# Selective scan on one core: VectorE multiplies the first unit of each block by C, and POOL multiplies whole units in one instruction

## What is computed

```python
x = x + 0.5 * ffn(layernorm(x))
h = layernorm(x)
for p in layers:                      # 4 layers
    xn = rmsnorm(h) * norm_w
    xp, z = split(xn @ Win)           # 256 channels each
    xc = silu(causal_conv(xp))
    dt, Bm, Cm = split(xc @ Wx)       # 64, 16, 16
    delta = softplus(dt @ Wdt + bdt)
    # over 512 steps, 256 channels x 16 states:
    s[t] = exp(delta[t] * A) * s[t-1] + (delta[t] * xc[t]) * Bm[t]
    y[t] = sum_over_states(s[t] * Cm[t]) + xc[t] * Dp
    h = h + (y * silu(z)) @ Wblk
x = x + h @ Wout + bout
x = x + 0.5 * ffn(layernorm(x))       # 8 experts, gate and up of 344 columns
```

## Time and profile before

| | us |
|---|---|
| median of 3 runs | 4576.21 (4574.02 to 4577.95) |
| profiled execution, its own time | 4581.88 |
| its span | 4580.2 |
| POOL busy in the span | 4095.2 (89%) |
| DVE busy | 4067.8 (89%) |
| PE busy | 3945.9 (86%) |
| ACT busy | 3346.7 (73%) |
| mean granted clock of PE | 0.948 of full |

### The profile page before, as it was taken

The page is one execution under the profiler, slowest core; times in us unless marked ns, Lnnn a source line. Parts: engine busy times, 40 slices in busy tenths (PEclk is TensorE's granted clock), DMA queues, the critical chain, the costliest instruction groups (busy, mean ns, idle before and its releaser), DMA issues.

```text
span 4580.2 us, 48320 instructions
## 1 busy us (share of the span) xinstructions
PE 3945.9 (86%) x11712; PEld 1285.4 (28%) x11712; DVE 4067.8 (89%) x5505; ACT 3346.7 (73%) x5047; POOL 4095.2 (89%) x1804
## 2 busy tenths in 40 slices
PE   7886777898998999899898999899899989678869
PEld 2221222232232323232232323223232322122223
DVE  2668898999999999999999999999999999889963
ACT  4566776777777787777778777787777777667744
POOL 0559999999999999999999999999999999999960
PEclk9897887999999999999999999999999999789969
DMA  2234444354435444544454445444434453443410
GB/s 72 58 74 96 112 100 94 88 114 104 94 90 111 97 94 96 114 95 94 98 111 93 89 105 113 92 91 104 111 87 92 109 113 85 98 100 88 93 46 5
DMA packets 137665, 426.06 MB, mean 93 GB/s; under 512 B 15917, under 2 KB 36334, under 8 KB 137007
## 3 DMA queue, kind: packets, MB, share of 16 engines
q1 hardware_dynamic: 137391, 422.97, 40.8%
HBM read 146.09 MB, written 8.39 MB: 34 GB/s over the span
## 4 chain that ended last, share of the span: by engine, by line
POOL 31%; DVE 25%; issue 17%; PE 16%; ACT 9%; DMA 1%; SPq 1%; DVEq 0%; ACTq 0%; POOLq 0%
POOL work L873 18%; POOL work L864 11%; DVE work L685 10%; DVE dA_ps L685 7%; PE d_ps L400 3%; ACT dA_ps L522 2%; DVE work L690 2%; PE a_ps L393 2%; DVE sg_sb L769 2%; ACT L550 2%; PE a_ps L387 2%; PE b_ps L387 1%; PE y_ps L371 1%; PE b_ps L393 1%; PE s_ps L470 1%
## 5 line engine op out<-in xcount | busy, mean ns | idle before, releaser
L873 POOL TENSOR_TENSOR work<-dd_sb,bc_sb 128x2048 f32<-128x2048 f32 x512 | 2318.8, 4529 | 127.1 <-PE y_ps L371 62.1
L522 ACT ACTIVATE dA_ps<-dd_sb,a_sb 128x512 f32<-128x512 f32 x2048 | 1370.7, 684 | 488.2 <-DVE work L690 298.0
L685 DVE TENSOR_TENSOR_SCAN work<-dA_ps,work 128x512 f32<-128x512 f32 x1408 | 1650.7, 1205 | 62.8 <-POOL work L873 36.6
L864 POOL TENSOR_TENSOR work<-work,bc_sb 128x1024 f32<-128x1024 f32 x704 | 1655.7, 2359 | 13.2 <-DVE work L685 11.9
L685 DVE TENSOR_TENSOR_SCAN dA_ps<-dA_ps,work 128x512 f32<-128x512 f32 x640 | 780.8, 1220 | 12.3 <-ACT dA_ps L522 6.1
L400 PE MATMUL d_ps<-sg_sb,wd_sb 128*128 128x512 f32 (+1 forms) x1536 | 728.7, 605 | 44.2 <-DVE sg_sb L769 44.2
L371 PE MATMUL y_ps<-work,sel_sum 128*32 128x512 f32 x4096 | 594.0, 654 | 88.6 <-POOL work L864 56.5
L387 PE MATMUL b_ps<-xT_sb,wg_sb 128*128 128x512 f32 (+1 forms) x768 | 433.9, 647 | 95.9 <-ACT sg_sb L549 91.8
L387 PE MATMUL a_ps<-xT_sb,wg_sb 128*128 128x512 f32 (+1 forms) x768 | 431.5, 644 | 97.1 <-ACT sg_sb L549 96.2
L690 DVE TENSOR_TENSOR work<-dA_ps,bc_sb 128x512 f32<-128x512 f32 x640 | 438.7, 685 | 11.8
L393 PE MATMUL a_ps<-xs_sb,wu_sb 128*128 128x512 f32 (+1 forms) x768 | 419.7, 629 | 20.4 <-DVE sg_sb L769 15.9
(11 more groups left out here) (116 smaller groups left out, 3820.7 us busy)
## 6 DMA issues: line engine op xcount, KB each, us to landing
dd_sb<-dd_src SPq DMA_DIRECT2D x512, 512.0 KB, 8.6
bc_sb<-bc_rows SPq DMA_DIRECT2D x256, 512.0 KB, 5.7
xr_sb<-in_L_attn_x SPq DMA_DIRECT2D x16, 256.0 KB, 2.8
bc_rows<-dbc_sb SPq DMA_DIRECT2D x128, 32.0 KB, 1.7
out<-xr_sb SPq DMA_DIRECT2D x16, 256.0 KB, 2.2
wg_sb<-in_L_ffn_Wg SPq DMA_DIRECT2D x1, 1376.0 KB
wu_sb<-in_L_ffn_Wu SPq DMA_DIRECT2D x1, 1376.0 KB
wd_sb<-in_L_ffn_Wd SPq DMA_DIRECT2D x2, 512.0 KB
```

The lines of the kernel that those rows point to most:

```text
L522: act.activation(dA_ps[:, g % NDA, :], dd_sb[:, b, c, 0, :], ACT.Exp, scale=a_sb[:, l, b, j, c:c + 1]).then_inc(dA_ready, 1)
L685: dve.tensor_tensor_scan(dA if on_dve(i) else tile, dA, tile, 0.0, ALU.mult, ALU.add).then_inc(scanned, 1)
L864: pool.tensor_tensor(work[:, g % RING], work[:, g % RING], bc_sb[:, j, 0, :].unsqueeze(1).broadcast_to([128, 2, T]), ALU.mult).then_inc(po ...
L873: pool.tensor_tensor(work[:, g % RING:g % RING + 2].rearrange("p h c t -> p (h c) t"), dd_sb[:, b, :, 1, :], bc_sb[:, j, 1, :].unsqueeze(1 ...
```

## The change

DVE now takes halves 0 and 1 (unit 0), 5 (second half of unit 2), 8 and 9 (unit 4): ten tiles as before. POOL multiplies units 1, 3, 5, 6 and 7 with one instruction of 128 x 2048 each, and half 4 with one of 128 x 1024. Units 0 and 4 have no POOL product. An instruction for a whole unit waits for all four scans of the unit, where one for a first half waited for two. All tables of offsets are new too; a few of their lines are shown.

```diff
-CORE = {"exp": -10, "scan": -1, "dbu": -1, "dve_prod": 0, "pool_prod": 17, "sum": 30, "y0": 87, "y1": 11}
+CORE = {"exp": -6, "scan": 0, "dbu": 7, "dve_prod": 3, "pool_prod": 27, "sum": 33, "y0": 92, "y1": 15}
...
-DVE_UNITS = (0, 2, 3, 5, 6)
-NDP, NPP = len(DVE_UNITS), HALVES - len(DVE_UNITS)
+DVE_HALVES = (0, 1, 5, 8, 9)
+POOL_HALVES = [[h for h in (2 * u, 2 * u + 1) if h not in DVE_HALVES] for u in range(UNITS)]
+NDP, NPP = len(DVE_HALVES), sum(1 for halves in POOL_HALVES if halves)
...
 def on_dve(i):
-    return i // NG in DVE_UNITS and i % NG >= 2
+    return i // 2 in DVE_HALVES
...
 def dve_products(k, i):
-    return k * NDP + sum(1 for u in DVE_UNITS if 2 * u + 1 <= i)
+    return k * NDP + sum(1 for h in DVE_HALVES if h <= i)
 def pool_products(k, i):
-    return k * HALVES + i + 1 - dve_products(k, i)
+    return k * NPP + sum(1 for halves in POOL_HALVES if halves and halves[-1] <= i)
...
-                if (at := part_at(t, CORE["pool_prod"], 8)) and not (at[2] % 2 == 1 and at[2] // 2 in DVE_UNITS):
-                    k, w, i = at
-                    j, g = (i // 2) % NJ, HALVES * k + i
-                    pool.wait_ge(scanned, 2 * g + 2)
-                    pool.tensor_tensor(work[:, g % RING], work[:, g % RING],
-                                       bc_sb[:, j, 0, :].unsqueeze(1).broadcast_to([128, 2, T]), ALU.mult).then_inc(pool_prod, 1)
+                if (at := part_at(t, CORE["pool_prod"], 16)) and POOL_HALVES[at[2]]:
+                    k, w, u = at
+                    halves = POOL_HALVES[u]
+                    h0, n = (HALVES * k + halves[0]) % RING, len(halves)
+                    tile = work[:, h0:h0 + n].rearrange("p h c t -> p (h c) t")
+                    pool.wait_ge(scanned, 2 * (HALVES * k + halves[-1]) + 2)
+                    pool.tensor_tensor(tile, tile, bc_sb[:, u % NJ, 0, :].unsqueeze(1).broadcast_to([128, 2 * n, T]),
+                                       ALU.mult).then_inc(pool_prod, 1)
```

More of the change, by code:

```diff
@@ L45 @@
-END = {"yt": 17, "xo": 30, "bn": 42, "nb": 69, "xtok": 67, "ht": 80, "h": 79, "store": 119, "acc": 9}
+CORE = {"exp": -6, "scan": 0, "dbu": 7, "dve_prod": 3, "pool_prod": 27, "sum": 33, "y0": 92, "y1": 15}
+PREP = {"dc1": 90, "dc0": 68, "sq": -23, "ms": -13, "rms": -8, "xn": -6, "xp0": 19, "conv0": 21, "xp1": 24, "conv1": 26,
+        "silu_xc": 30, "z0": 39, "zc0": 35, "z1": 51, "zc1": 53, "silu_z": 62, "wx": 43, "dbc": 43, "rows": 1, "dt0": 55,
+        "sp0": 59, "delta0": 62, "du0": 66, "dt1": 69, "sp1": 74, "delta1": 79, "du1": 86, "dd0": 21, "dd1": 110, "bc": 46}
@@ new lines @@
+NEAR = {"dc1": 110, "dc0": 89, "sq": 32, "ms": 37, "rms": 39, "xn": 43, "xp0": 53, "conv0": 54, "xp1": 56, "conv1": 58,
+        "silu_xc": 62, "z0": 65, "zc0": 65, "z1": 70, "zc1": 67, "silu_z": 94, "wx": 72, "dbc": 76, "rows": 23, "dt0": 76,
+        "sp0": 78, "delta0": 84, "du0": 84, "dt1": 91, "sp1": 91, "delta1": 97, "du1": 97, "dd0": 41, "dd1": 60, "bc": 33}
+POST = {"wblk": 93, "h": 92, "attn": 103, "x2": 108}
+POST_NEAR = {"wblk": 29, "h": 35, "attn": 38, "x2": 39}
+FFN_AT = {"gb": 1, "xs": 5, "g0": 7, "g1": 8, "g2": 11, "burst": 8, "u0": 14, "u1": 15, "u2": 18, "hh0": 15, "hh1": 17,
+          "hh2": 24, "down": 37}
@@ L48, in phase_table @@
+START = {"load": -130, "bn": -71, "nb": -46, "xtok": -46, "xt": -37, "xT": -38, "lg": -36, "lg_sb": -37, "mx": -36,
+         "mi": -36, "gap": -24, "we": -26, "eq": -26, "den": -15, "inv": -25, "comb": -8, "ct": -6, "gates": -14}
+END = {"yt": 25, "xo": 29, "bn": 46, "nb": 65, "xtok": 61, "ht": 87, "h": 87, "store": 102, "acc": 16}
 def phase_table():
```

## The result

The changed kernel takes 4788.24 us (4782.37 to 4791.23, three runs) against 4576.21 us: 1.0462 times as long, 95% interval 1.0446 to 1.0479. The forecast was 4750 us, with a range of 4590 to 4860. The profiled execution has a span of 4786.5 us, and in it POOL is busy for 4053.2 us (85%) and DVE for 4068.8 us (85%). DVE has the work that it had. POOL has 42 us less, nearly the 48 us that fewer instructions should save, and yet the kernel is 212 us slower.

A forecast was written before the change was run, and what follows sets the result against it. POOL set the pace, with DVE nearly as full; after the change a loop between them makes phases 68.0 us, 68.7 with the router, against 65.7. 58 x 3.0 = 174 us on 4576 gives 4750 us, range 4590 to 4860.

The forecast's parts named there:

- The bound before, and the gain: POOL sets the pace, DVE nearly as full; merged products save POOL 0.75 us a phase, 48 us over 64 phases.
- The loop: POOL from unit 5's product through unit 0's dbu, 18.2 us, then DVE's units 0 to 5, 49.8: 68.0 us.
- DVE's wait in front of unit 0: DVE waits for POOL's dbu before unit 0's first scan, about 3.0 us in each phase, where before it had none.
- The router term: Router steps on POOL delay unit 1's dbu by 1.6 us in every second phase, say 0.7 us a phase.
- The third rival: A sum in PE's queue waits for POOL's product, delaying expert matmuls; DVE has 3 us more a phase, 4942 us; chance 0.12.
- wrong if the time were in DVE's waits for PE: Sign in the changed profile that would refute the forecast: the time standing in DVE's waits for PE.
- The sum: Steady phases counted as 58 x 3.0 = 174 us more, added to 4576 us: 4750 us.
- The new tables for the start and the end I take as even: New offset tables at the program's start and end were counted as costing nothing.
- Sums in the shade: POOL's waits for PE's sums at dbu of units 6 or 2 fall within its scan waits; costed at nothing.

The follow-up runs named there:

- e3: Changed kernel, but POOL multiplies a whole unit in two instructions of 128 x 1024, the first waiting for two scans: 4711.95 us, 1.0315 to the kernel before.
- e8: Kernel before, its tables and division kept, with POOL's two products merged into one instruction in units 1, 4 and 7: 4765.63 us, 1.0409.
- e12: Kernel before with POOL's two products merged into one instruction in units 1 and 4 only, unit 7 keeping two: 4642.07 us, 1.0153.
- e1: Kernel before with all offset tables of the changed kernel, its division of products between DVE and POOL unchanged: 4719.14 us, 1.0337.
- e5: Changed kernel with a ring of eight halves instead of six, the up projection using the gate projection's weights for room: 4776.27 us, 1.0437.
- e9: Changed kernel with POOL's product of unit 6 and its sum 13 program steps later, behind the dbu of unit 0: 4889.02 us, 1.0671.
- e4: Changed kernel with a ring of eight halves, dbu 13 program steps earlier, and the up projection using the gate projection's weights: 5022.34 us, 1.0995.

## Why the prediction was right, and where it was off

*The bound before, and the gain (right).* The product of 128 x 2048 costs what `dbu` does: 4.53 us, next start 4.49 us later. POOL's busy time fell by 42 us, 0.13 us for each of 320 pairs, nearer the 48 us worked out from the rows than the 19 us set beside them. Nothing of it reached the end.

*The loop (right in place and size, in the phases where it closes).* 18.1 us measured for 18.2, 49.5 for 49.8, 67.7 for 68.0. But the two waits close a loop only in phases without a router, and this was the shortest of the four. e3 shows what waiting for four scans costs in the changed kernel: with the wait for two scans back, 1.4% return, of 4.6%. e8 and e12 show that merging costs in the kernel before too, by other waits.

*DVE's wait in front of unit 0, 3.0 us in each phase (half).* It is 3.2 us in the phases without a router and near nothing in those with one; 94 us in total between 600 and 4200 us, where I had announced some 150.

*The router term, 0.7 us a phase by a late d(1) (wrong place, too small).* d(1) wasn't late: DVE waits at unit 1 for 0.6 us in the whole stretch. I had taken the router's 3.5 us on POOL from the old order, and in the new one its first step stands in front of d(0). From p(5) to p(5) the four phases took 68.90, 69.25, 67.69 and 70.63 us, the second and fourth with the router in them; that is 1.6 us more on average in these. They have no wait for `dbu`; DVE loses the time to logits and `hh`. Over the four phases of the windows DVE's idle time grew by 14.2 us: 6.4 us for `dbu`, 6.5 more for `hh`, 2.5 more for logits, less small ones.

*The third rival, PE's order (much of its effect came, but not by its mechanism).* DVE's extra waits for PE are 9.0 us in four phases, over 2 us a phase, where the rival had 3 and the forecast at most its 0.7. But the rival's reason, a sum in PE's queue that waits for p(u), isn't in the trace: PE's matmuls wait 27.2 us for POOL's products between 600 and 4200 us, and 24.7 us before.

```profile
PE y_ps L371 <- POOL work L864: 24.7, 8, 7.9
PE y_ps L372 <- POOL work L867: 27.2, 6, 7.0
```

The forecast also said that it would be wrong if the time were in DVE's waits for PE. Half of it is.

*The sum (close, in part by luck).* From the first scan of the fifth phase to that of the sixty-first, a phase takes 68.63 us, and 65.57 us before: 3.1 us more for the 3.0 of the forecast, 171 us in 56 phases. (The four phases of the windows show 3.4; nearer both ends it is less.) That it is so near is luck: too much was announced for `dbu` and too little for PE, and the two made up for each other. The other 35 us of the 206 us between the two spans lie at the ends: the first scan comes 3.0 us later, the first four phases take 12.8 us more, the last four 5.9, and the part behind the last scan 13.3. The forecast had 6 us for both ends.

*"The new tables for the start and the end I take as even" (wrong).* This is the term behind those 35 us. In e1, which has the tables alone, the part behind the last scan is 164.4 us long, as in the changed kernel (164.7), and 151.4 us in the kernel before. For the steady phases the forecast priced no tables by themselves either. It read the order of POOL and DVE in the changed kernel as it is, tables and all, which is why the loop came out right, and of PE's order it read the sums alone. Yet e1 shows that most of the loss, 3.4 points of 4.6, comes with the tables.

*Sums in the shade (right).* POOL waits at d(6) in front of a longer wait at p(5). e3 shows the cover gone, and e5 that removing only the ring's wait gains next to nothing (1.0437 against 1.0462).

What stays open: why the tables cost 3.4%. By e1 they alone account for the 3.1% that e3 still loses, but the waits differ (e3 has 57.7 us for `dbu`, e1 21.7), and no run splits them into the router's chain on PE, POOL's waits for sums, and `eq`. The new division with the old tables and two instructions a unit was not run either. No version was found that beats the kernel before.

## What to carry to other kernels

One instruction for two can cost far more than a dispatch: it waits for the last of the inputs of both, and if the engines feed each other through a short ring, this wait can close a loop. Here it cost 1.5 points with the new tables, and 4.1 in the kernel before. Before merging, add up the loop (what stands on the producer between the merged instruction and the next item that the other engine needs, against what that engine has to do meanwhile), not the busy times. Read the order of every engine, and both ends of the program, before taking a new table as even. An order that was found for one division of the work says little about another: the same tables cost 3.4% with one and saved 8% with the other and its whole-unit instructions.

## What the runs showed of the hardware that I had not expected

A DVE instruction with both inputs in SBUF can be held up by a POOL instruction that runs beside it. The router's comparison `eq` reads `iota_e` and `mf_sb`, 128 x 32 elements. In the kernel before it took 163 to 194 ns each time. In e9, between 600 and 4200 us, and in e4:

```profile
L823 DVE TENSOR_TENSOR eq_sb<-iota_e,mf_sb 128x32 f32<-128x32 f32 x48 | 53.4, 1150 | 0.0
```

```profile
L815 DVE TENSOR_TENSOR eq_sb<-iota_e,mf_sb 128x32 f32<-128x32 f32 x48 | 177.2, 3729 | 0.0
```

DVE and POOL in e9 at such a place:

```profile
2337.53 4.68 DVE L823 TENSOR_TENSOR eq_sb<-iota_e,mf_sb 128x32 f32<-128x32 f32 x2
2342.14 0.16 DVE L828 RECIPROCAL wt_sb<-wt_sb 128x4 f32<-128x4 f32 x1
```

```profile
2337.66 8.97 POOL L880 TENSOR_TENSOR work<-work,bc_sb 128x2048 f32<-128x2048 f32 x2
```

The pair of comparisons ends at 2342.21, when the first of the two POOL products of 4.5 us does. The longest single one, 4557 ns in e9, is as long as one such POOL instruction. DVE's scans and products, which have one input in PSUM, show no such stretch: in e4 none of them takes longer than 1.23 and 0.69 us, as in the kernel before. The Trainium skill states this in "SBUF — State Buffer" (SBUF: two separate sides): a DVE instruction with two SBUF inputs and a GpSimd instruction that reads SBUF contend for a shared pair of ports; the one that starts first has it for its whole instruction, and the other is blocked. The trace agrees. In the changed kernel it costs little (226 ns on average), because `eq` mostly falls where one of POOL's large instructions is just ending; in e4, where it starts inside one, it took 177 us of the stretch, some 168 us more than at the 183 ns of the kernel before. It is one more reason why moving POOL's instructions against DVE's changes more than the waits on semaphores.
